# Mixture-of-experts layer behind cross attention, one core: gathers released by a table of needs, ten batches summed and stored by GpSimd, first tile turned ahead of the zero fills

## The reference

```python
x = x + xcond(layernorm(x), ctx, ctx, lengths)          # 8 heads
xt = layernorm(x)                                       # (2048, 512)
w, idx = top_k(softmax(xt @ gate.T), 2); w = w / w.sum()
y_e = (silu(xt @ w1[e].T) * (xt @ w3[e].T)) @ w2[e].T   # e = 0..7, 1024 inner channels
x = x + sum over the two chosen experts of w * y_e
```

## Time and profile before

| | us |
|---|---|
| median of 3 runs (lowest to highest) | 1244.6 (1242.59 to 1244.8) |
| the profiled execution | 1244.34 |
| its span | 1242.8 |
| attention and router | 0 to about 572 |
| last batch's router, tables, zero fills | about 572 to 591 |
| 37 tiles | 591 to 1190 |
| gathers, sums and stores | 1190 to 1242.8 |

### The profile page before, as it was taken

One profiled execution on the slowest core, in us unless ns is written; L12 is line 12 of the kernel. 1 busy time (PEld: TensorE's weight loads), 2 busy tenths in 40 slices (PEclk: granted clock), 3 DMA queues, 4 the chain that ended last, 5 costly groups with the idle time before them and its releaser, 6 DMA issues.

```text
span 1242.8 us, 19948 instructions
## 1 busy us (share of the span) xinstructions
PE 1071.0 (86%) x5113; PEld 419.8 (34%) x5114; DVE 817.7 (66%) x969; ACT 409.6 (33%) x734; POOL 617.0 (50%) x564
## 2 busy tenths in 40 slices
PE   1799999999999999861999999999999999999910
PEld 0223333333333333210444444444444444444400
DVE  5977877777777877313673864947768395953255
ACT  3266666666666666741111111110011101111100
POOL 6453666666666662123660752816657083840045
PEclk9999999999999999985999999999999999999965
DMA  6564555555555543013673755846657565753377
GB/s 172 161 216 149 169 156 158 158 164 161 164 164 164 164 135 102 21 37 109 200 166 87 216 144 143 220 93 194 168 178 178 142 186 146 215 134 83 71 226 257
DMA packets 210919, 191.65 MB, mean 154 GB/s; under 512 B 137376, under 2 KB 176288, under 8 KB 205472
## 3 DMA queue, kind: packets, MB, share of 16 engines
q1 hardware_dynamic: 196704, 119.86, 37.2%
q0 software_dynamic: 14176, 71.31, 17.5%
HBM read 107.50 MB, written 52.95 MB: 129 GB/s over the span
## 4 chain that ended last, share of the span: by engine, by line
PE 60%; POOL 11%; DMA 10%; DVE 7%; issue 6%; ACT 4%; POOLq 1%; SPq 1%; DVEq 0%; ACTq 0%
PE rows L1085 23%; PE heads_out L1085 12%; PE heads_out L999 7%; PE rows L972 6%; PE scores L986 6%; POOL W L429 6%; DMA W<-parts_dram 5%; ACT W L603 3%; DVE nm L720 3%; POOL W L428 3%; PE misc L1048 2%; DMA U<-expert_out_dram,fidx 2%; PE misc L1069 1%; PE misc L1025 1%; DMA U<-wpack_dram 1%
## 5 line engine op out<-in xcount | busy, mean ns | idle before, releaser
L1085 PE MATMUL rows<-W,U 128*128 (+1 forms) x1776 | 391.1, 380 | 23.4 <-DMA U<-stage 19.5
L720 DVE TENSOR_REDUCE nm<-rows 128x2 f32<-128x1024 f32 x256 | 305.3, 1219 | 59.6 <-PE rows L972 49.7
L603 ACT ACTIVATE W<-scores 128x512 f32<-128x512 f32 x512 | 282.7, 597 | 162.6 <-PE scores L986 157.2
L1085 PEld LDWEIGHTS rows<-W,U 128*128 128x128 bf16 x1776 | 174.1, 98 | 235.4 <-issue 29.3
L666 ACT ACTIVATE U<-rows 128x512 f32<-128x512 f32 x78 | 46.4, 597 | 517.8 <-PE rows L1085 509.0
L1085 PE MATMUL heads_out<-W,U 128*128 x888 | 197.8, 379 | 12.6 <-issue 10.2
L972 PE MATMUL rows<-W,U 96*128 96x512 bf16 x512 | 163.8, 404 | 49.2 <-DMA W<-parts_dram 28.1
L986 PE MATMUL scores<-U,W 128*128 128x512 bf16 x512 | 179.5, 386 | 14.0 <-ACT W L603 4.9
L429 POOL TENSOR_TENSOR W<-U,W 128x2048 bf16<-128x2048 f32 x42 | 172.4, 4104 | 7.7 <-POOL W L428 7.7
L910 DVE TENSOR_TENSOR U<-rows,U 128x512 f32<-128x512 f32 x78 | 53.5, 686 | 175.8 <-ACT U L666 175.8
L917 DVE TENSOR_TENSOR U<-U 128x512 bf16<-128x512 f32 x78 | 162.8, 2087 | 2.7
(11 more groups left out here) (150 smaller groups left out, 697.3 us busy)
## 6 DMA issues: line engine op xcount, KB each, us to landing
U<-wpack_dram POOLq DMA_DIRECT2D x42, 1024.0 KB, 5.8
parts_dram<-U SPq DMA_DIRECT2D x32, 384.0 KB, 4.1
U<-parts_dram SPq DMA_DIRECT2D x32, 384.0 KB, 4.0
W<-parts_dram SPq DMA_DIRECT2D x32, 384.0 KB, 5.5
stage<-slots_dram SPq DMA_DIRECT2D x39, 256.0 KB, 3.0
expert_out_dram<-U SPq DMA_DIRECT2D x39, 256.0 KB, 3.1
parts_dram<-U SPq DMA_DIRECT2D x32, 256.0 KB, 4.0
stage<-wpack_dram POOLq DMA_DIRECT2D x12, 512.0 KB, 5.3
```

The source lines that it names most:

```text
L603: s.activation(probs[:, w % 2, j, kk, :], sc[u % 2][:, :], ACT.Exp) \
L720: v.tensor_reduce(nm[:, bb.parity, 2 * k:2 * k + 2], p1[k % 2][:, :].rearrange("p (c k) -> p c k", c=2), AX_X, ALU.max, negate=True).then_ ...
L1085: ins = m.matmul(bank, part_of(s_part, k), W[:, bass.ds(at_w, 512)], start=(k == 0 and n == 0), stop=(k == n_chunks - 1 and n == 2))
```

## The change

Three things change.

1. Start of the expert stage. SyncE turns x of tile 0 before it waits for the zero fills. Row tiles 1 and 2 are loaded behind that wait, then tile 1 is turned. Four of the eight zero fills (odd experts) move from GpSimd to ScalarE's queue, behind its last activation of the tables.
2. A table of needs. Instead of the count of all needed tiles, VectorE works out for each batch how many tiles must have been stored: all those of experts 0 to 6, and of the last expert as many as hold its picks up to that batch. One more matmul (`last_counted`) sums the last expert's picks per batch over the partitions. The 13 steps of `stores_needed` run on VectorE between tiles 1 and 2. `btab` holds the two semaphore values for each batch.
3. The end. GpSimd's gather of batch b loads its two values from `btab` and waits for them, so it can run while later tiles are still computed. GpSimd itself does the sums of batches 0 to 9 (OWN = 10), with four instructions a batch in place of VectorE's two, and stores them. VectorE and SyncE keep batches 10 to 15.

```diff
@@ first tile and fills, SyncE, GpSimd, ScalarE
             sp.dma_start(xrow[:, 0, :], zs[0:P, :]).then_inc(xrow_in[0], 16)
-            sp.wait_ge(S["zero_out"], 16 * (1 + T - SURE + E))
+            turn_x(0, 0, first=True)
+            sp.wait_ge(S["zero_out"], 16 * (1 + T - SURE + E // 2))
+            sp.wait_ge(S["zero_act"], 16 * (E // 2))
             sp.wait_ge(S["tab_ready"], 1)
             load_row(1, 1)
-            for t in range(2):
-                turn_x(t, t, first=True)
-                load_row(t + 2, t)
+            load_row(2, 0)
+            turn_x(1, 1, first=True)
+            load_row(3, 1)
...
-            for e in range(E):
+            for e in range(0, E, 2):
                 r = pool.value_load(etab[0:1, 0, e:e + 1], min_val=0, max_val=E * REG - P)
                 pool.dma_start(zs[bass.ds(r, P), :], cv[:, :]).then_inc(S["zero_out"], 16)
...
+            act.wait_ge(S["cv_zero"], 1)
+            act.wait_ge(S["zero_ready"], 1)
+            for e in range(1, E, 2):
+                r = act.value_load(etab[0:1, 0, e:e + 1], min_val=0, max_val=E * REG - P)
+                act.dma_start(zs[bass.ds(r, P), :], cv[:, :]).then_inc(S["zero_act"], 16)
@@ SyncE's stores at the end
-            with sp.Fori(0, B) as b:
-                sp.wait_ge(S["comb_done"], b + 1)
+            with sp.Fori(OWN, B) as b:
+                sp.wait_ge(S["comb_done"], b - (OWN - 1))
@@ gathers, sums and stores on GpSimd
-            for par in range(2):
-                stored = pool.value_load(etab[0:1, 2, par:par + 1], min_val=16, max_val=16 * ((T + 1) // 2))
-                hold(y_out[par], stored)
+            hold(S["needs_ready"], 1)
+            hold(S["gates_ready"], 1)
+
+            def gather(b):
+                if b >= 4:
+                    if b - 4 < OWN:
+                        hold(S["own_done"], b - 3)
+                    else:
+                        hold(S["comb_done"], b - 3 - OWN)
+                for par in range(2):
+                    stored = pool.value_load(btab[0:1, par, b:b + 1], min_val=16, max_val=16 * ((T + 1) // 2))
+                    hold(y_out[par], stored)
                 for a in range(2):
                     pool.indirect_dma_start(
...
+            def combine(b):
+                hold(g_in[b % 4], b // 4 * 32 + 32)
+                xr, y0, y1 = xres[:, b, :], gb[:, b % 4, 0, :], gb[:, b % 4, 1, :]
+                for a, y in enumerate((y0, y1)):
+                    g.tensor_scalar(y, y, gate[:, a, b:b + 1], 0.0, ALU.mult, ALU.add).then_inc(S["own_steps"], 1)
+                hold(S["own_steps"], b * 3 + 1)
+                g.tensor_tensor(xr, xr, y0, ALU.add).then_inc(S["own_steps"], 1)
+                hold(S["own_steps"], b * 3 + 3)
+                g.tensor_tensor(xr, xr, y1, ALU.add).then_inc(S["own_done"], 1)
+
+            def put_out(b):
+                hold(S["own_done"], b + 1)
+                pool.dma_start(out[b:b + 1].rearrange("o p d -> p o d"), xres[:, b:b + 1, :]) \
+                    .then_inc(S["own_out"], 16)
 
             for b in range(B):
-                if b >= 4:
-                    hold(S["comb_done"], b - 3)
-                gather(b, b % 4)
+                gather(b)
+                if 2 <= b < OWN + 2:
+                    combine(b - 2)
+                if 3 <= b < OWN + 3:
+                    put_out(b - 3)
@@ VectorE's tables: two steps added, four removed
+            link(v.tensor_tensor(last_b[:, :], c3[:, 0:2 * B:2, E - 1], c3[:, 1:2 * B:2, E - 1], ALU.add))
+            v.nop().then_inc(S["last_ready"], 1)
...
-            link(v.tensor_scalar(count_t, tio[:, 0, 1:T + 1], cum[:, E - 1:E], None, ALU.is_le))
-            for par in range(2):
-                link(v.tensor_reduce(counts2[:, par:par + 1], count_t[:, par:T:2], AX_X, ALU.add))
-            link(v.tensor_scalar(etab[:, 2, 0:2], counts2, 16.0, None, ALU.mult))
+            link(v.tensor_copy(before_last[:, :], cum[:, E - 2:E - 1]))
@@ VectorE, between tile(1) and tile(2)
+            def stores_needed():
+                order = tio[:, 0, 0:B]
+                dve.wait_ge(S["last_counted"], 1)
+                link(v.tensor_tensor(until, order.unsqueeze(2).to_broadcast([P, B, B]),
+                                     order.unsqueeze(1).to_broadcast([P, B, B]), ALU.is_ge))
+                link(v.tensor_tensor(until, until, sc[0][:, 0:B].unsqueeze(1).to_broadcast([P, B, B]), ALU.mult))
+                link(v.tensor_reduce(cum_b, until, AX_X, ALU.add))
+                link(v.tensor_tensor(until, cum_b.unsqueeze(2).to_broadcast([P, B, B]),
+                                     tio[:, 1, 0:B].unsqueeze(1).to_broadcast([P, B, B]), ALU.is_gt))
+                link(v.tensor_reduce(need_b, until, AX_X, ALU.add))
+                link(v.tensor_scalar(need_b, need_b, before_last[:, 0:1], None, ALU.add))
+                link(v.tensor_copy(odd_i, need_b))
+                link(v.tensor_scalar(odd_i, odd_i, 1, None, ALU.bitwise_and))
+                link(v.tensor_copy(odd_b, odd_i))
+                for par, op in enumerate((ALU.add, ALU.subtract)):
+                    link(v.tensor_tensor(parts_b, need_b, odd_b, op))
+                    link(v.tensor_scalar(btab[:, par, :], parts_b, 8.0, None, ALU.mult))
+                v.nop().then_inc(S["needs_ready"], 1)
@@ VectorE's sums: the loop over 16 batches becomes 10 to 15, unrolled
-            with dve.Fori(0, B // 4) as i:
-                for r in range(4):
-                    b = i * 4 + r
-                    dve.wait_ge(g_in[r], i * 32 + 32)
+            for b in range(OWN, B):
+                dve.wait_ge(g_in[b % 4], b // 4 * 32 + 32)
```

More of the change, by code:

```diff
@@ L74, in build @@
     SURE = 2 * TOK // P
+    OWN = 10
     CH = 1024
@@ L160, in build @@
         tab = sb("tab", [P, 4, T + 1], I32)
-        etab = sb("etab", [P, 3, E], I32)
+        etab = sb("etab", [P, 2, E], I32)
+        btab = sb("btab", [P, 2, B], I32)
+        last_b = sb("last_b", [P, B], BF16)
+        before_last = sb("before_last", [P, 1], F32)
         fidx = sb("fidx", [P, B, 2], I32)
@@ L171, in build @@
         at_base = small[:, 256:256 + 2 * B]
-        count_t, counts2 = small[:, 320:320 + T], small[:, 384:386]
+        until = norm[:, 0:B * B].rearrange("p (b k) -> p b k", k=B)
+        cum_b, need_b, odd_b, parts_b = (rest[:, n * B:(n + 1) * B] for n in range(4))
+        odd_i = rest[:, 4 * B:5 * B].bitcast(I32)
         hb = U[:, 0:1024].bitcast(BF16).rearrange("p (n s i) -> p n s i", n=2, s=2)
@@ L374, in _ @@
             store_tile(T - 1, 0)
-            with sp.Fori(0, B) as b:
-                sp.wait_ge(S["comb_done"], b + 1)
+            with sp.Fori(OWN, B) as b:
+                sp.wait_ge(S["comb_done"], b - (OWN - 1))
                 sp.dma_start(out[bass.ds(b, 1)].rearrange("o p d -> p o d"), xres[:, bass.ds(b, 1), :]) \
                     .then_inc(S["out_done"], 16)
-            sp.wait_ge(S["out_done"], 16 * B)
+            sp.wait_ge(S["out_done"], 16 * (B - OWN))
+            sp.wait_ge(S["own_out"], 16 * OWN)
         @block.gpsimd
@@ L558, in _ @@
                     expert(e, par)
-            for par in range(2):
-                stored = pool.value_load(etab[0:1, 2, par:par + 1], min_val=16, max_val=16 * ((T + 1) // 2))
-                hold(y_out[par], stored)
-            def gather(b, r):
+            hold(S["needs_ready"], 1)
[9 more added lines that the diff above has]
+                    hold(y_out[par], stored)
                 for a in range(2):
                     pool.indirect_dma_start(
-                        out=gb[:, r, a, :], out_offset=None, in_=ys[:, :],
+                        out=gb[:, b % 4, a, :], out_offset=None, in_=ys[:, :],
                         in_offset=bass.IndirectOffsetOnAxis(ap=fidx[:, b, a:a + 1], axis=0)) \
-                        .then_inc(g_in[r], 16)
-            for b in range(B):
-                if b >= 4:
-                    hold(S["comb_done"], b - 3)
-                gather(b, b % 4)
+                        .then_inc(g_in[b % 4], 16)
+            def combine(b):
[11 more added lines that the diff above has]
+                    .then_inc(S["own_out"], 16)
+            for b in range(B):
+                gather(b)
[3 more added lines that the diff above has]
+                    put_out(b - 3)
         @block.scalar
@@ L891, in _ @@
             link(v.tensor_tensor(gate[:, 1, :], gexp[:, :], gate[:, 0, :], ALU.mult))
+            v.nop().then_inc(S["gates_ready"], 1)
             def take_y(t, par, early=False):
@@ L926, in _ @@
             tile(1, 1, early=True)
+            stores_needed()
             tile(2, 0, early=True)
@@ L936, in _ @@
             v.nop().then_inc(S["comb_steps"], 1)
-            with dve.Fori(0, B // 4) as i:
-                for r in range(4):
-                    b = i * 4 + r
-                    dve.wait_ge(g_in[r], i * 32 + 32)
-                    xr = xres[:, bass.ds(b, 1), :].rearrange("p o q -> p (o q)")
```

(15 more changed lines are left out.)

2 lines of the change are left out of this document (1 added, 1 removed).

## The result

The changed kernel takes 1254.3 us in the median of five executions (1251.6 to 1260.8), the kernel before 1244.1 beside it: a ratio of 1.010, with an interval from 1.007 to 1.013. It is slower by 1% (the medians themselves lie 0.8% apart). The profiled execution took 1251.6 with a span of 1250.0, so it lies 2.7 under its median; the predicted span of 1252.0 is to be set against that 1250.0.

What follows compares the result with a forecast made beforehand. TensorE was the chain through the expert stage; after the change GpSimd would bound the tail. Span 1253.0 less 1.0 is 1252.0; with 1.5 over the span and 0.3 to the median, 1253.8 us, range 1240 to 1264.

Steps and rivals of the forecast that it cites:

- The prediction's 36 us: Tail: time gained by starting the gathers early, said to be more than eaten by sums, stores and register loads.
- Part 1, first matmul: Start of the expert stage: TensorE begins tile 0 at 585.5, 5.9 us earlier, the split fills taken as free.
- Part 1, what is late next: Tile 0's first down product: follows GpSimd's expert 1, so 4.2 us earlier, between 3.5 and 5.9.
- Part 2: Needs table on VectorE between tiles 1 and 2: GpSimd blocks steps, making tile 3 3.2 us late, bounds 0 to 4.9.
- Rival B: Needs chain slips between GpSimd's instructions or costs nothing, 4 to 6 us of the early start stay: 1250; chance 0.14.
- Parts 1 and 2 together: Early start and needs table combined: 1.0 us earlier, between 5.9 earlier and 1.4 later.
- Part 3, the cycle: GpSimd's tail: sums, store and gathers cost 8.4 to 8.5 us per own batch, where before a batch cost 2.5.
- C: One batch's sums on GpSimd: two scalings, two sums and their waits, 4.45 us.
- The last three batches: Batches 13 to 15, end of GpSimd's tail: gathers with register loads at 3.3 us each.
- The start: Tail: the fourth batch's gathers wait for tile 33 and end at 1157.1, before subtracting the 1.0 us shift.
- G3: The fourth batch's two gathers on GpSimd, waiting for tile 33, predicted to end at 1157.1.
- Rival A: GpSimd prepares loads and gathers beside its own sums: cycle 7.1 to 7.6 us, time 1238 to 1245; chance 0.22.

Runs made afterwards that it cites:

- own7: Changed kernel with OWN = 7 in place of 10; 1238.3 us, ratio 0.996 to the kernel before.
- part1_alone: Kernel before with only tile 0's x turned ahead of the wait and four zero fills on ScalarE; 1244.8 us, ratio 0.9985.
- fills_pool: Changed kernel with all eight zero fills back on GpSimd; 1259.4 us, ratio 1.011 to the kernel before.
- turn_only: Kernel before with only tile 0's x turned ahead of the wait, all eight fills left on GpSimd; 1241.2 us, ratio 0.997.
- const_waits: Changed kernel with the 32 register loads for the gathers' waits replaced by constants; 1253.4 us, ratio 1.005 to the kernel before.
- best7: Changed kernel with OWN = 7, the 13 needs steps ahead of tile 0 and all fills on GpSimd; 1234.6 us, ratio 0.990 to the kernel before.
- best5: Changed kernel with OWN = 5, the 13 needs steps ahead of tile 0 and all fills on GpSimd; 1229.6 us, ratio 0.989 to the kernel before.
- fills_pool_late: Changed kernel with all fills on GpSimd and expert 1 held until tile 0's h is turned; 1260.7 us, ratio 1.011 to the kernel before.
- turn_late: Kernel before with tile 0's x turned ahead of the wait and expert 1 held until tile 0's h is turned; 1240.9 us, ratio 0.997.
- best7_late: best7 with expert 1 held until tile 0's h is turned; 1231.4 us, ratio 0.989 to the kernel before.

## Why the prediction was right, and where its steps were not

The sign, the size and the reason held: GpSimd becomes the bound of the tail, and the earlier start does not pay for ten times 5.2; own7, with three own batches fewer, shows it. (The prediction's 36 us set the fourth batch after against the first batch before. Batch for batch the start is 42.8 earlier and the rest 49.9 longer; its sum did not use the 36.) How near the numbers came is partly luck. In the span of 1252.0 against 1250.0 errors of opposite sign cancel: the fourth batch's gathers ended 2.6 later than predicted, the nine cycles took 2.8 less and the way from there to the last gather 1.9 less. And the predicted median of 1253.8 against 1254.3 has a second such pair: the profiled execution lay 2.7 under its median, not 0.3.

- Part 1, first matmul: predicted 585.5, measured 586.60. Of the 1.1 some 0.4 is the attention stage's later end. The rest I see in the load of tile 0's rows, issued at 577.37 and with ScalarE 4.5 later, where it was 2.9 before; it is 4.4 to 4.5 in the five kernels with this part and the new tables, 4.0 in part1_alone, and 2.9 to 3.2 in all with the fills on GpSimd. The fills on ScalarE were not quite free for this load. The turn behind it is 0.4 shorter with them, though (3.30 to the first matmul in the kernel after, 3.72 in fills_pool), so that fills_pool gains only 0.4 at the first matmul; with the old tables, which hold x of tile 0 until later, part1_alone (14.6) is ahead of turn_only (15.3).
- Part 1, what is late next: the step was right that GpSimd's expert 1 sets the first down product. It was sized at 4.2, and 2.4 came: GpSimd's expert 1 itself was 2.5 earlier (593.99, predicted 592.3), and L955 of tile 0 was held for its full 4.48. That the fills' split itself brings the two together I did not see; the trace of turn_only shows it. And of the earlier start 0.25 goes with the lower clock, the first 96 matmuls taking 22.96 instead of 22.71 (0.57 and 0.63 in their first 5 us).
- Part 2: the chain lasted 14.15, predicted some 14. The loss was 4.9 at the down product behind tile 3's up products (first down product 2.4 earlier, this one 2.6 later than before), which is the upper bound and not the 3.2 that I took: TensorE waited twice for VectorE, once per half of tile 3, and I had counted one. Rival B falls. On the sentence from the Trainium skill ("SBUF — State Buffer", "Who interferes with whom"): the trace agrees that reductions pass (L967, 0.42, in the middle of L438) and that two SBUF inputs are held (L968, 3.32). I had concluded that this makes only three steps blockable; by their form it is four (L964, L968, L976 twice). But the same section also counts `tensor_scalar` among the operations that can contend when their operands allow it, and the rows agree: L971 2.38, L973 4.00. The rule taken whole speaks for a loss at the upper end, not at the low one.
- Parts 1 and 2 together: predicted 1.0 earlier, and about 1.5 later was measured (tile 32's up product at 1103.13 instead of 1101.68, of which 0.4 is the attention stage). This error is 2.5 to the slow side, 0.4 of it from the attention stage.
- Part 3, the cycle: predicted 8.4 to 8.5. C came to 4.0 instead of 4.45, the sums at 1.25 instead of 1.276 and the scalings 1.36 for two; the gathers with their loads 3.05 instead of 3.3, of which const_waits gives 0.5 to the loads. Undisturbed, the cycle is 7.67. Four of the nine were longer (8.31, 9.45, 8.37, 9.07), so that the mean is 8.19. The 9.45 holds the gap of 2.07 in front of a gather; in the other ones the scalings took up to 2.07 for two instead of 1.36. Three of the four lie between 1173 and 1199, where VectorE still works on tiles 35 to 38, which fits the two engines holding each other up, but I didn't isolate it.
- The last three batches: predicted 3.3 each, measured 3.5 for the first with the last store in front of it and 2.5 to 2.6 for the others, with the loads hidden beside the gathers ahead. From the gathers of batch 12 to the last gather it is 9.9 instead of 11.8, 1.9 to the fast side. The nine cycles, 73.7 instead of 76.5, make another 2.8.
- The start: G3 at 1156.47, its second gather's end at 1158.7. Predicted 1157.1 for that end, less 1.0, so 2.6 late; the shift of parts 1 and 2, 2.5 beyond the predicted one, explains it. The last gather to the end: 9.9, predicted 9.8.
- Rival A was nearer than I thought: const_waits has its cycle, 7.2, and is still not faster, since the tail starts later than rival A took it to, and four of its cycles are of 7.4 to 8.0. What turns the sign is OWN: at 7 the kernel is 0.4% faster than before.

## What to carry to other kernels

Work moved from the last engine of a tail to one that also issues the tail's transfers is paid at its full length once the idle time is used up: count how many such units fit in the time gained (here at a price of 5.2 us each, against 42.8 us, so eight), and move no more. Seven, below that bound, made the kernel faster than before; at five the other engine's queue decided. Releasing a background engine earlier can cost the foreground one its undisturbed moment; ask when the result is needed, and release it then. Put a chain of small dependent VectorE steps where GpSimd computes nothing, whatever their sum alone says: the same 13 steps took 4.0 us there and 14.15 beside GpSimd's split.

## What I had not expected of the hardware

- Two VectorE steps of 16 elements per partition with one SBUF tensor as input were held for 2.38 and 4.00 us by GpSimd's instructions, against 0.23 and 0.17 alone (L971, L973); reductions, and a two-input step with one operand in PSUM (L966, 0.42), were not.
- A DMA transpose issued just ahead of two 1 MB weight loads went with very slow loads: 14.96 us when the turn was 0.45 ahead (fills_pool), 10.61 at 0.53 ahead (best7), 7.44 at 0.12 ahead (best5), 5.2 to 6.3 where the load was held until the turn had landed (fills_pool_late, turn_late, best7_late), and 4.1 to 4.8 where the load went first (all the others). These are single executions, and the distance alone does not order them; which share is the turn's own is open.
- GpSimd's register loads take 0.29 each here and start beside its own compute instruction; of a pair 0.5 us stays visible where nothing disturbs it. The Trainium skill's "DMA: Bandwidth & Descriptors", "Latency and other measured facts", has a floor of about 600 ns for a `tensor_load`, without saying from which memory; the rows of after (from SBUF) and the difference to const_waits stay below it.
